# Two query tiles share a value pass, and joins and norms move a turn, in the first attention of a two-layer block

## What is computed

```python
Q = xn @ Wq ; K = ctx @ Wk ; V = ctx @ Wv            # heads of 128, one head
attn = softmax(Q @ K.T / sqrt(128))
out  = (attn @ V) @ Wo + bo + xn
out  = out @ Wfc
out  = layernorm(out) * gamma + beta
x    = x + out
```

## Time and profile before

| | |
|---|---|
| median of 3 runs | 1105.44 us |
| profiled execution | 1107.57 us, its span 1105.6 us |
| TensorE busy | 1026.7 us (93%) |
| VectorE, ScalarE, GpSimd busy | 64%, 46%, 36% of the span |
| mean granted TensorE clock | 0.963 of full speed |
| first scores of the first attention | 46.37 us into the span |
| last logits kept by VectorE | 213.65 us |
| first matmul of the experts after it | 217.46 us |

### The profile page before, as it was taken

The page is one execution under the profiler, slowest core; times in us unless marked ns, Lnnn a source line. Parts: engine busy times, 40 slices in busy tenths (PEclk is TensorE's granted clock), DMA queues, the critical chain, the costliest instruction groups (busy, mean ns, idle before and its releaser), DMA issues. The chain is left out here.

```text
span 1105.6 us, 19661 instructions
## 1 busy us (share of the span) xinstructions
PE 1026.7 (93%) x7166; PEld 954.2 (86%) x7166; DVE 702.8 (64%) x1651; ACT 514.0 (46%) x1061; POOL 399.4 (36%) x645
## 2 busy tenths in 40 slices
PE   5999998599799999995999999999999999999983
PEld 4899998488799999995877889999999999999982
DVE  5577776366588888883657545544445666666762
ACT  4446665323466666662244533333344444444441
POOL 5324455407223332222732100000004867767540
PEclk9999999599999999997999999999999999999995
DMA  7200000201377778883311310000000111111000
GB/s 217 77 1 1 1 1 1 76 1 58 102 208 238 235 237 239 236 223 114 95 39 58 115 29 1 20 1 1 1 1 11 22 28 30 30 30 29 11 10 10
DMA packets 57529, 78.54 MB, mean 71 GB/s; under 512 B 5680, under 2 KB 37552, under 8 KB 57456
## 3 DMA queue, kind: packets, MB, share of 16 engines
q1 hardware_dynamic: 38896, 50.04, 15.1%
q0 software_dynamic: 16304, 24.91, 8.2%
q10 hardware_dynamic: 2256, 2.62, 0.7%
HBM read 62.61 MB, written 14.94 MB: 70 GB/s over the span
## 5 line engine op out<-in xcount | busy, mean ns | idle before, releaser
L40 PE MATMUL bank<-V_hi,XT_lo 128*128 128x256 f32 x416 | 123.6, 297 | 1.2 <-DVE XT_lo L2001 1.2
L2001 DVE TENSOR_TENSOR XT_lo<-bank,XT_lo 128x512 fp32r<-128x512 f32 x116 | 73.3, 633 | 77.8 <-ACT XT_lo L1694 77.2
L1694 ACT ACTIVATE XT_lo<-bank 128x512 fp32r<-128x512 f32 x116 | 63.9, 553 | 119.0 <-PE bank L1453 118.4
L42 PE MATMUL bank<-V_hi,XT_lo 128*128 128x256 f32 x416 | 117.1, 281 | 0.0
L41 PE MATMUL bank<-V_lo,XT_lo 128*128 128x256 f32 x416 | 116.9, 281 | 0.0
L40 PE MATMUL bank<-rx_hi,expert_w_hi 128*128 128x256 f32 x368 | 106.4, 289 | 2.5 <-PEq L846 2.5
L42 PE MATMUL bank<-rx_hi,expert_w_lo 128*128 128x256 f32 x368 | 104.7, 284 | 0.0
L41 PE MATMUL bank<-rx_lo,expert_w_hi 128*128 128x256 f32 x368 | 104.5, 284 | 0.0
L2006 DVE TENSOR_REDUCE part<-wide 128x1 f32<-128x402 f32 (+1 forms) x116 | 72.4, 624 | 38.7 <-PE wide L42 36.7
L406 DVE TENSOR_TENSOR expert_w_lo<-sraw,expert_w_hi 128x1024 fp32r<-128x1024 f32 x72 | 88.0, 1222 | 13.4 <-ACT expert_w_hi L402 13.3
L40 PE MATMUL wide<-expert_w_hi,XT_hi 128*128 128x402 f32 (+1 forms) x232 | 91.4, 394 | 3.4 <-issue 2.4
(11 more groups left out here) (414 smaller groups left out, 3302.9 us busy)
## 6 DMA issues: line engine op xcount, KB each, us to landing
sraw<-w1T SPq DMA_DIRECT2D x25, 512.0 KB, 5.4
sraw<-w3T SPq DMA_DIRECT2D x25, 512.0 KB, 5.1
sraw<-w2T SPq DMA_DIRECT2D x25, 512.0 KB, 3.9
routed_results<-rys POOLq DMA_DIRECT2D x23, 256.0 KB, 4.4
XT_hi<-queries POOLq DMA_DIRECT2D x16, 256.0 KB, 3.3
X<-x ACTq DMA_DIRECT2D x4, 512.0 KB, 7.5
token_rows<-Fx SPq DMA_DIRECT2D x4, 512.0 KB, 4.9
out<-X SPq DMA_DIRECT2D x16, 128.0 KB, 1.7
```

Of the source, the lines that this page charges most:

```text
L40: pe.matmul(out, wh, xh, start=first, stop=False)
L42: return pe.matmul(out, wl, xh, start=False, stop=last)
L1694: act.activation(weights(g, nk, 0), transposed(g, nk), ACT.Copy).then_inc(sem["high"], 1)
L2001: dve.tensor_tensor(weights(g, nk, 1), transposed(g, nk), weights(g, nk, 0).bitcast(F32), ALU.subtract).then_inc(sem["low"], 1)
```

## The change

1. The value product. The transposed probabilities `pt` get three slots instead of two: slot 0 holds the high part of an even query tile, slot 1 that of an odd one, slot 2 the low part of the tile in work. An even tile's `weighted` makes only V high x [high | low] (13 matmuls of 256 columns). An odd tile's makes the same 13, and 13 of V low x [high of the even tile | high of the odd tile] into the other 256 columns of the bank (26 matmuls). V low x probabilities low is no longer made at all.
2. ScalarE's `finish` of an odd tile copies 384 columns instead of 128 into `sums`. A new GpSimd step `add_low`, in odd turns between the two `inverse`s, waits for `summed` and adds the two low sums to the `cx` of both tiles of the pair (two 128x128 additions); `split` waits for them (`pair_added`).
3. Since an even tile is complete only when its odd partner is, stages 3 to 5 (`join` with `split`, the first norm with `add`, the second norm with tokens and logits) of tiles 0 to 14 come one turn later. Tile 15 keeps its turns, so turns 18, 19 and 20 have the stage of tile 14 and then that of tile 15.
4. The second buffer of probabilities now lies in `sraw` (`raw`), so SyncE waits for the last transposes (`t_done` at 64) before it loads the expert's weights there.

```diff
-                prob = sb(ctx, "a0prob", [P, 2, nk * P])
-                pt = sb(ctx, "a0pt", [P, nk, 2, P], F32R)
+                probs = (sb(ctx, "a0prob", [P, nk * P]), raw[:, 0:nk * P])
+                pt = sb(ctx, "a0pt", [P, 3, nk, P], F32R)
...
-                blk.sync(on_sync)
+                @blk.sync
+                def _(sp):
+                    sp.wait_ge(t_done, nq * G)
+                    start_loads(sp)
...
+                def at(t, stage):
+                    return [j for j in (t - stage - 1,) if 0 <= j < nq - 1] + [nq - 1] * (t - stage == nq - 1)
...
                         for k in range(4 * g, min(4 * g + 4, nk)):
-                            both = pt[:, k, :, :].rearrange("p h n -> p (h n)")
-                            pe.matmul(ob[:, 0:2 * P], V_hi[:, k, :], both, start=k == 0, stop=False)
-                            m = pe.matmul(ob[:, 0:2 * P], V_lo[:, k, :], both, start=False, stop=k == nk - 1)
+                            high_and_low = pt[:, 1:3, k, :] if odd else pt[:, 0:3:2, k, :]
+                            m = pe.matmul(ob[:, 0:2 * P].rearrange("p (h n) -> p h n", n=P), V_hi[:, k, :], high_and_low,
+                                          start=k == 0, stop=k == nk - 1 and not odd)
+                            if odd:
+                                m = pe.matmul(ob[:, 2 * P:4 * P].rearrange("p (h n) -> p h n", n=P), V_lo[:, k, :],
+                                              pt[:, 0:2, k, :], start=False, stop=k == nk - 1)
...
                         if j >= 3:
-                            pe.wait_ge(kept, j - 2)
+                            pe.wait_ge(kept, min(j, nq - 2) - 2)
+                        if j == nq - 1:
+                            pe.wait_ge(added, nq - 1)
...
-                        pe.wait_ge(added, min(j + 3, nq))
+                        pe.wait_ge(added, j + 3 if j + 4 < nq else nq)
                         pe.wait_ge(normal2, j + 1)
-                        if j + 2 >= nq:
+                        if j + 3 >= nq:
                             pe.wait_ge(kept, j)
...
-                            if g == 0 and real(i - 3):
-                                join(i - 3)
-                            if g == 1 and real(i - 5):
-                                turn_tokens(i - 5)
-                            if g == 3 and real(i - 5):
-                                logits(i - 5)
+                            if g == 0:
+                                for j in at(i, 3):
+                                    join(j)
+                            if g == 1 and at(i, 5):
+                                turn_tokens(at(i, 5)[0])
+                            if g == 3 and at(i, 5):
+                                logits(at(i, 5)[0])
+                                for j in at(i, 5)[1:]:
+                                    turn_tokens(j)
+                                    logits(j)
...
-                        act.activation(sum_lo[:, :], ob[:, P:2 * P], ACT.Copy).then_inc(f_act, 1)
+                        if i % 2:
+                            if i > 1:
+                                act.wait_ge(pair_added, i - 1)
+                            act.activation(sums[:, :], ob[:, P:4 * P], ACT.Copy).then_inc(f_act, 1)
+                        else:
+                            act.activation(sums[:, 0:P], ob[:, P:2 * P], ACT.Copy).then_inc(f_act, 1)
...
+                    def add_low(i):
+                        pool.wait_ge(summed, i + 1)
+                        for h in range(2):
+                            pool.tensor_tensor(cx[:, h, :], cx[:, h, :], sums[:, (h + 1) * P:(h + 2) * P], ALU.add)\
+                                .then_inc(pair_added, 1)
+
                     def split(j):
-                        pool.wait_ge(summed, j + 1)
+                        pool.wait_ge(pair_added, 2 * (j // 2) + 2)
...
                     for i in range(turns_all):
-                        if real(i - 3):
-                            split(i - 3)
-                        if real(i - 4):
-                            add(i - 4)
-                        if real(i - 3):
-                            inverse(i - 3, MV, RSTD, SHIFT, stat1, inv1)
-                        if real(i - 4):
-                            inverse(i - 4, MV2, R2, H2, stat2, inv2)
+                        for j in at(i, 3):
+                            split(j)
+                        for j in at(i, 4):
+                            add(j)
+                        for j in at(i, 3):
+                            inverse(j, MV, RSTD, SHIFT, stat1, inv1)
+                        if real(i - 2) and i % 2:
+                            add_low(i - 2)
+                        for j in at(i, 4):
+                            inverse(j, MV2, R2, H2, stat2, inv2)
```

More of the change, by code:

```diff
@@ L1041, in high @@
                         act.wait_ge(t_done, i * G + g + 1)
-                        act.activation(weights(g, 0), transposed(g), ACT.Copy).then_inc(thi, 1)
+                        act.activation(weights(g, i % 2), transposed(g), ACT.Copy).then_inc(thi, 1)
                     def exponent(i, half):
@@ L1072, in _ @@
                     for i in range(turns_all):
-                        if real(i - 4):
-                            normalise(i - 4)
-                        if real(i - 5):
-                            normalise_again(i - 5)
+                        for j in at(i, 4):
+                            normalise(j)
+                        for j in at(i, 5):
+                            normalise_again(j)
                         if real(i - 1):
@@ L1082, in _ @@
                             high(i - 1, 1)
-                        if real(i - 5):
-                            token_high(i - 5)
+                        for j in at(i, 5):
+                            token_high(j)
                         if real(i):
@@ L1164, in finish @@
                             dve.wait_ge(cx_split, i - 1)
[L1165 removed]
+                        dve.tensor_tensor(cx[:, i % 2, :], ob[:, 0:P], sums[:, 0:P], ALU.add).then_inc(summed, 1)
                         dve.wait_ge(inv_done, 2 * i + 1)
@@ L1217, in _ @@
                             keep_features(5)
[L1218 to L1223, removed]
+                        for j in at(i, 3)[:1]:
+                            partial(j, Fx, added, stat1)
+                        for j in at(i, 5)[:1]:
+                            token_low(j)
+                        for j in at(i, 3)[:1]:
+                            aggregate(j, MV, stat1)
+                        for j in at(i, 3)[1:]:
+                            partial(j, Fx, added, stat1)
+                            aggregate(j, MV, stat1)
                         if real(i - 1):
@@ L1227, in _ @@
                             keep_features(6)
-                        if real(i - 4):
-                            partial(i - 4, X, residual, stat2)
+                        for j in at(i, 4)[:1]:
+                            partial(j, X, residual, stat2)
                         if real(i - 2):
                             finish(i - 2)
-                        if real(i - 4):
-                            aggregate(i - 4, MV2, stat2)
+                        for j in at(i, 4)[:1]:
+                            aggregate(j, MV2, stat2)
+                        for j in at(i, 4)[1:]:
+                            partial(j, X, residual, stat2)
+                            aggregate(j, MV2, stat2)
                         if real(i - 1):
@@ L1237, in _ @@
                             keep_features(7)
-                        if real(i - 5):
-                            keep_logits(i - 5)
+                        for j in at(i, 5)[:1]:
+                            keep_logits(j)
+                        for j in at(i, 5)[1:]:
+                            token_low(j)
+                            keep_logits(j)
         def first_row(i):
```

26 lines of the change are left out of this document (14 added, 12 removed).

## The result

The changed kernel takes 1111.21 us (median of 5 runs, 1108.95 to 1111.87) against 1104.03 of the kernel before beside it. The ratio is 1.0052, with a 95% interval of 1.0034 to 1.0071: slower by 4 to 8 us, on the very edge of what a measurement of this kernel tells from no change. The forecast was 1110.0 with a range of 1101 to 1117.

What follows compares the result with a forecast made beforehand. The prediction saw TensorE busy in inner turns, with a second chain through high 1 and token_low ending in the same place. Gains of 2.9 us and a tail of 7.3 made +4.4 us: 1110 us, range 1101 to 1117.

Steps and rivals of the forecast that it cites:

- The sum: Whole program: 2.9 us gained by turn 17 and 7.3 lost in the last turns, together +4.4 us.
- turn 16: First attention: keeps its 8.98 us, because it waited for GpSimd already.
- last stretch: From the value product of tile 15 to the last logits kept; forecast 7.3 us longer.
- What is removed: Value product: 13 matmuls fewer per even turn, 1.53 us less of TensorE, 12.3 us over eight turns at most.
- An even turn: Inner turns with the short value product: 0.21 us shorter, not 1.53; the rest becomes TensorE waits.
- An odd turn: Inner turns with all 26 value matmuls: 8.55 us, no change.
- The early turns: Turns 2 to 6: stages coming a turn later gain about 0.4, 0.1 and 0.46, then 1.1 us in turns 5 and 6.
- even turns lower the clock: Rival, chance 0.08: waits in even turns start odd turns at 1.2 GHz, 10 to 15 us on top, 1120 to 1125.
- a clock under 1.00 before turn 17: Sign in TensorE's granted clock that the prediction said would prove it wrong.
- The last turns: Tile 14 goes ahead of tile 15 from cx to the last logits: +7.3 us, bounds 4 and 10.
- SyncE's: Three loads moved behind the last transposes: hidden by the tail; without it they would cost up to 5.4 us.
- the rule of the Trainium skill: Elementwise additions belong on VectorE: the two additions there would end 0.3 us sooner; sum not touched.

Runs made afterwards that it cites:

- Experiment 2: Kernel before with V's low part left out of every tile, no shift and no additions: ratio 0.9876 (0.9841 to 0.9912).
- Experiment 4: Changed kernel with GpSimd's two additions moved behind the second inverse: ratio 1.0063 (1.0040 to 1.0085).
- experiments 6 and 9: 6: changed kernel with VectorE's token_low ahead of the first statistics, 1.0048. 9: kernel before with that and own banks for tiles 13 to 15, 0.9990.
- experiment 3: Changed kernel with tiles 14 and 15 making their own four products and keeping their old turns: ratio 1.0009 (0.9988 to 1.0030).
- experiment 8: Changed kernel with additions on VectorE, token_low first and own banks for tiles 13 to 15, run twice: 0.9974 and 0.9984.
- Experiment 1: Changed kernel with every tile making all four products and no additions, so the shift alone: ratio 1.0041 (1.0015 to 1.0068).
- experiment 7: Changed kernel with a bank each for join, turned tokens and logits of tiles 13 to 15: ratio 1.0025 (1.0008 to 1.0043).
- Experiment 5: Changed kernel with the pair's two additions on VectorE after the odd tile's cx, none on GpSimd: ratio 1.0032 (1.0017 to 1.0048).

## Why the prediction was right

**The sum.** Forecast: +4.4 us; the stage in the profile: +6.9; the ratio: 3.8 to 7.8. Sign and mechanism were right and the size came out near, 2.5 us too low in the profile. The parts, with gains positive, are these:

| | forecast | measured |
|---|---|---|
| gained when turn 16 starts | 2.9 | 2.4 |
| turn 16 | 0 | -1.3 |
| last stretch | -7.3 | -7.9 |

**What is removed** held: 104 matmuls, and almost nothing of them reached the time. Experiment 2 shows why: even where nothing takes their place, a turn gives back 0.64 of 1.53 us.

**An even turn** was forecast at 8.33 us and took 8.50 (8.48 to 8.50), so it is only 0.04 us shorter than before and not 0.21; turns 8 to 14 gave 0.2 us together, not 0.8. The walk was right from step to step and 0.13 short at one of them: the `inverse` started at 2.13 of the turn and not at 2.00, 0.09 after the second addition's end and not 0.42 after its start as `add` did behind `split` before (123.31 and 123.73). From there all is late by that much or a little more: `normalise_again` 3.41 for 3.27, join 4.20 for 4.07, `high` 1 5.77 for 5.61, logits 7.81 for 7.64. Experiment 4 shows which of the two paths counts: the join's.

**An odd turn** was forecast at 8.55 and took 8.55, but "TensorE bounds it" was true only to a tenth (experiments 6 and 9: 8.44). The columns in two runs cost nothing that shows. The copy of 384 columns took 0.49 on ScalarE, 0.22 more than 128, and cost nothing in an inner turn.

**The early turns** came out as walked: turns 2, 3 and 4 gave 0.49, 0.16 and 0.63, turn 5 took 7.28, turn 6 9.26 (9.1 forecast). Together turns 2 to 6 gave 2.2 us where 2.1 was forecast, so the head start at turn 16 is theirs and hardly the even turns'.

**Turn 16 is the step that failed.** "Turn 16 (8.98) keeps its length: it waited for GpSimd already." It took 10.31 us instead of 8.98. The join came 0.85 later in it, at 4.19, since GpSimd has two additions more before it; that wait was in my walk for inner turns and I took it as hidden here. With it TensorE had no work between the transposes of group 0, which end at 179.5, and 181.39; then the clock stood at 0.50 (1.2 GHz) from 182.3 to 185.5. The rival "even turns lower the clock" had the right kind of cost and the wrong place: turns 8, 10, 12 and 14 with a wait of 0.65 us each, and turn 6 with one of 1.40, kept 1.00, and turn 16, which has no scores, did not. That the wait before the join alone did it isn't borne out. In experiment 3, with the same additions and the join at 4.20 of the turn but with 26 value matmuls, turn 16 kept the full clock and took 9.82: the wait by itself costs 0.8 of the 1.3 us. In experiment 2, with 13 value matmuls and no additions, the clock fell. All five kernels with 26 value matmuls in turn 16 kept the clock, and six of the seven with 13 lost it. The exception is the version of experiment 8, which kept it in both profiles and took 8.94; why isn't isolated. So the runs point to the shorter value product itself, together with the waits, as what cost turn 16 its clock. The prediction had named a clock under 1.00 before turn 17 as what would prove it wrong: on this point it did, at a price of 1.3 us with the wait in it, and turn 17 started 1.0 us sooner after the first scores instead of about 3.

**The last turns** were forecast at 7.3 and took 7.9 more. Join of 15: forecast 2.5 later, measured 2.7 from the product's start. First norm (ScalarE's L1083): 4.0 later, forecast 3.7. GpSimd's `add`: 5.5 for 5.0. `normalise_again`: 5.5 for 5.0. The end: 7.9 for 7.3. From `cx` of tile 15 to the end it took 24.3 us, where the prediction named some 24, at a clock of 0.50 as before. Experiment 1 shows that this comes from the shift alone, experiment 7 that 3.8 us of it hang on the one bank that two tiles share.

**SyncE's** loads landed under the last turns: DMA moved 206 GB/s in the window from 187.51 on and nothing in the one from 195.06 on, and ScalarE's first use of them came after 220. Nothing waited for them: the first matmul of the experts came 3.81 us after the last logits, as before.

The prediction named, as a remark that doesn't touch the sum, the rule of the Trainium skill (GPSIMD Engine Reference, section Engine selection) to put elementwise additions on VectorE. Experiment 5 does so. An even turn then gave 0.37 us, near the 0.3 us that I worked out there, and the stage some 2 us. The price doesn't vanish: on VectorE the additions hold up the statistics that the `inverse` waits for.

## What to carry to other kernels

An engine that is 99% busy in a stage can still have a second chain that ends with it: read, for each engine, how long its last awaited instruction had ended before it started, and take at most that slack as the gain. A pipeline stage moved one turn later pays at the end, where two tiles go through queues and a bank made for one; cost those last turns instruction by instruction. New work on a side engine costs what stands behind it in that engine's queue, not its own duration, and this holds on the engine that it is moved to as well. Before an edit is credited with what a stage gained, look at the granted clock of each part: here 2.3 of 4.3 us were clock.

## What the runs showed of the hardware that was not expected

- The clock in the last turns is not the same from run to run of one kernel: the version of experiment 8 ran the value product of tile 15 up to `cx` in 5.77 us at 1.00 in one profile and in 7.31 at 0.77 in the other. That alone moves the stage by 1.5 us, a good part of what is compared here. In the inner turns, at full clock throughout, the two profiles agree to 0.03 us a turn.

```profile
183.49:189.26 5.77, 4.75 (x37) 4.47 (x37) 2.08 (x10) 2.08 (x4) 3.49 (x9) 1.00 0.73 267
```

```profile
183.06:190.37 7.31, 6.28 (x37) 5.99 (x37) 2.13 (x10) 2.08 (x4) 3.94 (x10) 0.77 0.58 210
```

- Two chips differed by 1.6% (1121 and 1104 us) for the same kernel, and not evenly: the inner turns of this stage are the same on both, the parts behind it took 898 to 903 us on the one and 883 to 889 on the other. Only ratios to the kernel beside compare.
